# A scan re-ordered by pairs of heads, one convolution tap moved to ScalarE and GpSimd, and a re-ordered opening

## The reference

```python
zxbcdt = u @ in_proj_w.T                      # z 256, x 256, B 2048, C 2048, dt 32 columns
xBC = causal_conv1d(xBC, conv_w, conv_b)      # depthwise, 4 taps: y[l] = sum_k w[k] * x[l - 3 + k] + b
a_log = -softplus(dt); cum = cumsum(a_log)
seg = exp(cum_i - cum_j)
scores = where(tril, seg * einsum('in,jn->ij', C, B), 0)
y = scores @ x                                # per head; plus the state carried between chunks of 128
y = y + D * x;  out = (y * silu(z + z_bias)) @ out_proj_w.T
```

## Time and profile before

| | us |
|---|---|
| median of 3 runs | 1198.76 (1198.08 to 1199.36) |
| the profiled execution's own time | 1198.02 |
| its span, first to last instruction | 1196.3 |

### The profile page before, as it was taken

One profiled execution on the slowest core, in us unless ns is written; L12 is line 12 of the kernel. 1 busy time (PEld: TensorE's weight loads), 2 busy tenths in 40 slices (PEclk: granted clock), 3 DMA queues, 4 the chain that ended last, 5 costly groups with the idle time before them and its releaser, 6 DMA issues.

```text
span 1196.3 us, 18801 instructions
## 1 busy us (share of the span) xinstructions
PE 1043.1 (87%) x6632; PEld 634.3 (53%) x6632; DVE 847.9 (71%) x1864; ACT 518.6 (43%) x1125; POOL 251.7 (21%) x519
## 2 busy tenths in 40 slices
PE   3999898798999898988999998998998998976556
PEld 1444445554444656654444666654445576555345
DVE  4999724578999665678999646789998546765138
ACT  1766521246766311446666211446665212421134
POOL 3222100032222010132221011132221001224432
PEclk9999999899999999999999999999999999988778
DMA  5789400002434000004333000004336304034546
GB/s 191 262 272 278 146 1 18 1 2 92 133 119 127 11 1 19 18 2 133 120 126 102 2 0 18 19 5 160 122 120 175 94 1 124 2 93 117 182 148 233
DMA packets 74255, 113.27 MB, mean 95 GB/s; under 512 B 5944, under 2 KB 64192, under 8 KB 73266
## 3 DMA queue, kind: packets, MB, share of 16 engines
q1 hardware_dynamic: 70322, 100.08, 27.0%
q10 hardware_dynamic: 2304, 8.39, 2.0%
q0 software_dynamic: 1536, 3.60, 1.0%
HBM read 93.38 MB, written 19.27 MB: 94 GB/s over the span
## 4 chain that ended last, share of the span: by engine, by line
PE 60%; DVE 20%; issue 8%; ACT 7%; POOL 2%; another core or an unknown queue 1%; DMA 1%; DVEq 0%; POOLq 0%; SPq 0%; ACTq 0%
PE bank L902 24%; DVE hf L1688 6%; PE bank L967 4%; PE bank L1145 3%; PE bank L1053 3%; PE bank L1187 3%; PE bank L1069 3%; DVE u L1924 2%; PE bank L915 2%; PE bank L1231 2%; PE bank L1234 2%; PE bank L982 2%; PE bank L893 2%; POOL rs L1536 2%; PE bank L1286 1%
## 5 line engine op out<-in xcount | busy, mean ns | idle before, releaser
L902 PE MATMUL bank<-uT,w_in 128*128 128x512 f32 (+1 forms) x584 | 284.2, 614 | 15.9 <-DVE hf L1688 11.5
L1688 DVE SCALAR_TENSOR_TENSOR hf<-bank,conv_w,hf 128x510 f32<-128x510 f32 (+2 forms) x384 | 277.7, 743 | 16.4 <-ACT hf L1392 11.1
L902 PEld LDWEIGHTS bank<-uT,w_in 128*128 128x128 f32 (+1 forms) x584 | 99.7, 187 | 112.1 <-issue 78.5
L1392 ACT ACTIVATE hf<-bank,conv_b,conv_w 128x512 f32<-128x512 f32 x128 | 99.3, 776 | 135.2 <-PE bank L902 135.2
L1536 POOL TENSOR_TENSOR rs<-ve,half 128x2 f32<-128x2 f32 x56 | 38.9, 695 | 305.5 <-DVE ve L1824 305.3
L1053 PE MATMUL bank<-hf 64*128 64x256 f32 x512 | 90.3, 429 | 12.6 <-issue 7.2
L902 PE MATMUL bank<-uT,w_gu 128*128 128x512 f32 x224 | 99.0, 593 | 0.0
L2108 DVE TENSOR_REDUCE nmax<-bank 128x2 f32<-128x256 f32 (+1 forms) x128 | 65.4, 553 | 20.3 <-PE bank L1234 18.1
L1372 ACT ACTIVATE xc<-bank 128x512 f32<-128x512 f32 x44 | 26.3, 597 | 117.4 <-PE bank L902 77.1
L1053 PEld LDWEIGHTS bank<-hf 64*128 64x128 f32 x512 | 39.1, 186 | 69.9 <-issue 63.6
L1924 DVE TENSOR_TENSOR turned_p<-dec,bank 128x768 f32<-128x768 f32 x64 | 60.9, 952 | 15.9 <-PE bank L1054 4.8
(11 more groups left out here) (306 smaller groups left out, 2050.9 us busy)
## 6 DMA issues: line engine op xcount, KB each, us to landing
hf<-cum_dram SPq DMA_DIRECT2D x32, 384.0 KB, 3.6
dec<-cum_dram SPq DMA_DIRECT2D x32, 384.0 KB, 3.6
tmp<-cum_dram SPq DMA_DIRECT2D x32, 384.0 KB, 3.5
x<-cum_dram SPq DMA_DIRECT2D x32, 384.0 KB, 3.5
y_dram<-xf SPq DMA_DIRECT2D x16, 512.0 KB
hf<-y_dram ACTq DMA_DIRECT2D x16, 512.0 KB, 4.9
w_in<-in_w_in SPq DMA_DIRECT2D x1, 3584.0 KB, 11.7
w_in<-in_w_egu SPq DMA_DIRECT2D x6, 512.0 KB, 9.3
```

The source lines that it names most:

```text
L902: mm = pe.matmul(plan[key][0:n, :], w[:, k, cols], uT[:, k, :], start=k == 0, stop=k == DC - 1)
L1392: act.activation(dst, plan[key][:, :], ACT.Identity, bias=conv_b[:, j:j + 1], scale=conv_w[:, j, TAPS - 1:TAPS]).then_inc(tap0.sem, 1)
L1688: ins = dve.scalar_tensor_tensor(d, x, conv_w[:, j, TAPS - 1 - s:TAPS - s], d, ALU.mult, ALU.add)
```

## The change

Scan. TensorE goes by pairs: the products of both sequences, both projections of pair p + 2, and behind an odd pair both `add_y`. VectorE does the C taps of pair p + 1 ahead of the first multiplication of pair p, and the B taps of pair p + 2 behind the second. For C chunks of pairs 2 to 14 the last tap (s = 3) leaves VectorE: ScalarE writes w[0]·x to a buffer `last_product` (`tap_product`), and GpSimd adds it to `bc` once VectorE is done with taps 1 and 2; VectorE's tap 2 then drains the bank (`tap_and_drain`). TensorE waits for that add before it uses the chunk. Pair 15 keeps three taps on VectorE.

Opening. GpSimd clears `x_pad`, `before` and `table` before the powers, the others behind u. The two halves of u are turned into banks 6 and 7. VectorE clears `zeros_bf` first, and TensorE multiplies zeros 16 times before it turns u. ScalarE runs one small exponential at once (so that its table is loaded), and the waits for `consts_cast` come later.

```diff
         for j in range(2):
-            plan.use(("T", "mix", j), 6, -1)
+            plan.use(("T", "mix", j), 6 + j, -1)
...
             pe.wait_ge(consts_in, 144)
+            pe.wait_ge(*plan.before(("T", "mix", 0), -1))
+            pe.wait_ge(zeros_ready, 1)
+            pe.wait_ge(ahead_var.sem, ahead_var.at(0, 1))
+            for n in range(16):
+                pe.matmul(plan.of(("T", "mix", 0), -1)[:, :], zeros_bf[:, 0:P], zeros_bf[:, :], start=True, stop=True)
             for j in range(2):
                 transposes(pe, "mix", 0, u, j, -1)
-            pe.wait_ge(consts_cast, 1)
...
-                for g in range(2 * PAIRS):
+                def states_times_queries(g):
...
+                for p in range(PAIRS):
+                    for w in range(2):
+                        if p < PAIRS - 1:
+                            pe.wait_ge(*plan.drained(("BC", p, w), r))
+                            if w == 1 and p >= 2:
+                                pe.wait_ge(conv_sum.sem, conv_sum.at(r, p - 1))
                     if p + 2 < PAIRS:
-                        if p + 2 == PROJ_PAIRS[1] and b == 0:
+                        for b in range(2):
+                            states_times_queries(2 * p + b)
+                        if p + 2 == PROJ_PAIRS[1]:
                             pe.wait_ge(w_proj[2], 16)
-                        project_bc(p + 2, b)
+                        for w in range(2):
+                            project_bc(p + 2, w)
+                        if p % 2 == 1:
+                            for b in range(2):
+                                add_y(p, b)
...
+            act.wait_ge(pads_zero, 1)
+            act.activation(empty[:, 0:TILES], half[:, :], ACT.Exp)
             for j in range(2):
                 turned("mix", j, -1, 2)
+            softplus(0)
             act.wait_ge(consts_cast, 1)
-            softplus(0)
...
+                def tap_product(p):
+
+                    key = ("BC", p, 1)
+                    if p > 2:
+                        act.wait_ge(conv_sum.sem, conv_sum.at(r, p - 2))
+                    x = plan[key][:, :].rearrange("p (b l) -> p b l", b=SEQS)[:, :, 0:SEQ - TAPS + 1]
+                    act.activation(last_product, x, ACT.Copy, scale=conv_w[:, 18 + p, 0:1]).then_inc(tap3.sem, 1)
...
                         first_tap(("BC", p + 2, b), bc[:, (p + 2) % 3, b, :], 2 + 16 * b + p + 2)
+                        if b == 1 and p + 2 < PAIRS - 1:
+                            tap_product(p + 2)
...
+                    p = g // 2
+                    if g % 2 == 1 and 2 <= p < PAIRS - 1:
+
+                        pool.wait_ge(tap3.sem, tap3.at(r, p - 1))
+                        pool.wait_ge(*plan.drained(("BC", p, 1), r))
+                        settle(pool)
+                        x = bc[:, p % 3, 1, :].rearrange("p (b l) -> p b l", b=SEQS)[:, :, TAPS - 1:SEQ]
+                        pool.tensor_tensor(x, x, last_product, ALU.add).then_inc(conv_sum.sem, 1)
...
+                def all_taps(p, w):
+                    if w == 1 and p < PAIRS - 1:
+                        dve.wait_ge(tap3.sem, tap3.at(r, p - 1))
+                        tap(r, 1, [bc_chunk(p, w)], taps_done)
+                        tap_and_drain(r, 2, *bc_chunk(p, w))
+                        return
+                    for s in range(1, TAPS):
+                        tap(r, s, [bc_chunk(p, w)], taps_done)
```

More of the change, by code:

```diff
@@ L389, in sandwich @@
         pads_zero = sem("pads_zero")
+        zeros_ready = sem("zeros_ready")
         PADS = 7
@@ L1074, in add_y @@
                                           skip_group_check=True).then_inc(y_added.sem, 1)
-                for g in range(2 * PAIRS):
+                def states_times_queries(g):
                     p, b = steps[g]
[L1078 to L1081, removed]
                     pe.wait_ge(*plan.before(("CB", p, b), r))
-                    for second in [products(n) for n in ns]:
+                    for second in [products(n) for n in (2 * g, 2 * g + 1)]:
                         mm = second()
                     mm.then_inc(plan.fills(("CB", p, b)), 1)
+                for p in range(PAIRS):
[4 more added lines that the diff above has]
+                                pe.wait_ge(conv_sum.sem, conv_sum.at(r, p - 1))
                     if p + 2 < PAIRS:
-                        if p + 2 == PROJ_PAIRS[1] and b == 0:
+                        for b in range(2):
+                            states_times_queries(2 * p + b)
+                        if p + 2 == PROJ_PAIRS[1]:
                             pe.wait_ge(w_proj[2], 16)
-                        project_bc(p + 2, b)
-                    if g == 1:
+                        for w in range(2):
[3 more added lines that the diff above has]
+                                add_y(p, b)
+                    else:
+                        b = p - (PAIRS - 2)
+                        for i in range(2):
+                            g = 2 * (PAIRS - 2) + 2 * b + i
+                            if b == 0 and i == 1:
+                                for w in range(2):
+                                    pe.wait_ge(*plan.drained(("BC", PAIRS - 1, w), r))
+                            states_times_queries(g)
+                            if b == 1 and i == 0:
+                                add_y(*steps[g - 1])
+                    if p == 0:
                         for c in range(DC):
@@ L1695, in tap, with tap_and_drain @@
                         ins.then_inc(plan.drains(key), 1)
+            def tap_and_drain(r, s, key, dst, j):
+                dve.wait_ge(chain, last_tap[0])
+                d = dst.rearrange("p (b l) -> p b l", b=SEQS)[:, :, s:SEQ]
+                x = plan[key][:, :].rearrange("p (b l) -> p b l", b=SEQS)[:, :, 0:SEQ - s]
+                dve.scalar_tensor_tensor(d, x, conv_w[:, j, TAPS - 1 - s:TAPS - s], d, ALU.mult, ALU.add)\
+                    .then_inc(plan.drains(key), 1)
             last_tap = [0]
@@ L1916, in _ @@
                     p, b = steps[g]
+                    d = 2 * g % 4
+                    if g % 2 == 0 and 1 <= g // 2 <= PAIRS - 2:
+                        all_taps(g // 2 + 1, 1)
                     dve.wait_ge(decayed.sem, decayed.at(r, 2 * g + 2))
@@ L1928, in _ @@
                         tap(r, TAPS - 1, [bc_chunk(1, w) for w in range(2)], taps_done)
[L1929 to L1933 removed]
+                    if g % 2 == 1 and g // 2 + 2 < PAIRS:
+                        all_taps(g // 2 + 2, 0)
                 output(1, slice(SEQ, GROUP), 64)
```

33 lines of the change are left out of this document (15 added, 18 removed).

## The result

| | us | ratio to before, 95% interval |
|---|---|---|
| before, median of 3 | 1198.76 (1198.08 to 1199.36) | |
| changed kernel, median of 4 | 1161.36 (1159.64 to 1164.04) | 0.9688 [0.9675, 0.9701] |
| forecast | 1165 (1154 to 1181) | |

The changed kernel is 3.1% faster, 37.4 us by these medians (37.2 when before's fourth run, 1198.43, is counted).

The account below looks back on a forecast made before the run. TensorE was taken as the bound, VectorE as a near second. From 1198.02 us, 25.8 for the scan and 7.5 for the opening left 1164.7; with 0.7 for the median 1165.4, say 1165, range 1154 to 1181.

Parts of the forecast that it names:

- Scan, the stretch: Four scan steps (two pairs of heads), bound by TensorE, fall from 13.04 to 11.92 us, 1.12 less.
- a sign of being wrong: In the scan, a four-step stretch above 12.4 us would show the forecast wrong; 11.6 to 12.1 was expected.
- Scan, the ends: First stretch and last pairs (14 and 15) of each scan round: nothing together, bounds −1 and +1 us a round.
- Scan, round 0's DMA: Round 0's scan would want 1.06 of the DMA engines, so 1 us was taken off the gain, bounds 0 and 5.
- ScalarE's loop: Scan, per pair: product, two taps, multiplication, exponentials, next first tap, hand-overs make 5.6 of 5.96 us; 0.35 to spare.
- Opening: Before the scan: earlier u, zeros, table load and second bank gain 7.5 us, bounds 4.8 and 9.6.
- buys the full clock for what follows: Opening: zeros delay u's turning by 2 us but let the first projections take 3.46 instead of 6.32.
- (a): Scan: GpSimd's add blocks VectorE, which needs 13.3 us a stretch; scan gives nothing or −7, total 1198; chance 0.07.
- (b): Scan: ScalarE's product and added semaphores lengthen the 5.6 us loop by 0.6; stretch 12.5, total 1178; chance 0.20.
- (c): Opening: clock not up after the zeros, gain 4.8 us, total 1168; counted inside the forecast's 0.66.
- (d): Scan: GpSimd's add takes over 4.4 us (point of decision), kernel slower than before, about 1233 at 5; chance 0.03.
- (e): Opening gains nothing, as the power's library load stands behind three clears; total 1172, inside the forecast's 0.66.

Follow-up runs that it names:

- pool_x2: Changed kernel with GpSimd adding the product twice in two dependent steps, so the result holds it twice; 1167.18 us, ratio to before 0.9721.
- act_x2: Changed kernel with ScalarE writing the product twice, the second after the first is done; 1176.96 us, ratio to before 0.9833.
- no_zeros: Changed kernel without the products of zeros in the opening; 1144.24 us on the third chip, where before took 1178.89; ratio 0.9704.
- pool_x3: Changed kernel with GpSimd doing add, subtract, add in place of one add, same result; 1198.29 us, ratio to before 1.0002.
- after_again: The changed kernel, unaltered, run once more on the third chip; 1143.12 us where before took 1178.89, ratio 0.9688.
- last_too: Changed kernel with pair 15's C chunk also getting its last tap by ScalarE and GpSimd; 1147.2 us on the third chip, ratio 0.9717.

## Why the prediction was right, and which terms were off

**Scan, the stretch: right.** 11.92 was forecast, 11.89 came, and the chain has the pieces of the sum: a pair of product groups 1.51 (forecast 1.58), eight projections 3.81 and 3.63 (3.65 each), two `add_y` 1.44 (1.46). The experiments bear out that both parts are needed for it: 12.32 and 12.84 with one alone. One stretch a round breaks the forecast: the one with the half of y takes 12.43, above the 12.4 that I had named as a sign of being wrong, and TensorE waits for a tap in it. I had taken the six stretches as alike. It costs 0.54 a round, where before lost 0.21 at the same place.

**Scan, the ends: mis-sized.** I took them as nothing. In round 1, from the first products to the first `add_y`, before took 12.92 and after 11.81, so the first stretch gained 1.1 as well, just above the upper bound of 1; the next six gave 6.6 (forecast 6.7: five gave 1.15 each instead of 1.12, the sixth less), the end nothing.

**Scan, round 0's DMA: wrong sign of caution.** I took 1 us off. My step was that the same bytes in less time would want 1.06 of the DMA engines. A window of round 0 shows them at 0.98 with 309 GB/s, where before had 0.97 with 280, and TensorE without a gap. So the busy share was no measure of the room left:

```profile
82.00:98.00 16.00, 16.00 (x131) 9.00 (x124) 14.70 (x21) 12.51 (x30) 7.11 (x14) 1.00 0.98 309
```

pool_x2 shows that the caution had its place: with 1.4 us more on GpSimd the same rows of cum hold TensorE up.

**What I had no term for: the clock at the end of the scan.** TensorE waits 1.9 us there for pair 15's taps (in before 1.81); VectorE's last of six taps in a row ends at 368.03, TensorE goes on at 368.14. Behind the wait the granted clock sometimes falls. The same group in round 1 and in round 2 of the changed kernel, timelines of TensorE:

```profile
370.16 0.64 PE L1079 MATMUL bank<-turned_p,x_pad 128*32 128x256 f32 x8 [0.29 <-DVE turned_p L1991]
...
624.09 1.08 PE L1079 MATMUL bank<-turned_p,x_pad 128*32 128x256 f32 x8
```

The window 624 to 628 has a granted clock of 0.64, 370 to 374 has 1.00. The changed kernel had the fall in rounds 2 and 3, before in round 0 alone: its second group of products there takes 1.13 (timeline of before), in round 1 0.63.

```profile
139.36 1.13 PE L1053 MATMUL bank<-hf 64*128 64x256 f32 x4
```

That is what sets round 0 (8.87 saved) and rounds 2 and 3 (6.4, 6.65) off from round 1 (7.71): with the fall a scan is 1.1 to 1.3 longer. In sum the four scans gave 29.6 instead of 25.8.

**VectorE, ScalarE, GpSimd: right.** VectorE 10.74 (10.6 to 10.9), ScalarE 9.59 (10.2 at most), the product 0.67 (0.6 to 0.8), the add 1.27 (1.2). "Up to about 2.5 us cost nothing": two adds, 2.7 with the hand-over, cost nothing in round 1's regular stretch but 5.5 us over the four scans. "The stretch reaches 13.04 again only with an add of about 4": 13.2 at 4.17. ScalarE's loop was called the tightest. act_x2 shows that a loop through ScalarE is, with 0.72 more per stretch for 1.38 more work in it, so 0.66 were covered (forecast 0.35 a pair, 0.7). That these agree is partly luck: the loop that its chain shows has TensorE's projections in it in place of VectorE's multiplication.

**Opening: right to 0.75, partly for the wrong reason.** 7.5 forecast, 8.25 came. u ended at 12.7 and the zeros at 14.0 instead of 14.7. The projections started at 15.4, not 16.7, and took 4.13, not 3.46. Both parts of my step "buys the full clock for what follows", and then 3.46, were off. The 3.46 was misread, for that row in round 3 is not of the same shape. It belongs to the feed-forward's first projections (`w_gu`), which all write 128 rows. On the timeline of before it reads:

```profile
929.12 3.62 PE L915 MATMUL bank<-uT,w_gu 128*128 128x256 f32 x16
```

Those of the opening go by fours between 32 rows (dt) and 128 (x). At the full clock their fours start 0.95, 1.06 and 0.98 apart, against 0.87 in round 3, and this is most of what lies between 3.62 and 4.13. And the clock did not have to be bought. The weight loads show the clock, one after another; the granted clock of the windows reads 1.00 throughout. First before, the timeline of the weight loads:

```profile
23.25 1.36 PEld L915 LDWEIGHTS bank<-uT,w_in 128*128 128x128 f32 x4 [0.81 <-issue]
...
26.66 0.73 PEld L915 LDWEIGHTS bank<-uT,w_in 128*128 128x128 f32 x4 [0.41 <-issue]
```

The changed kernel, inside its zeros, which start 0.43 apart up to 12.17 and 0.21 apart from 12.55:

```profile
12.17 0.15 PEld L952 LDWEIGHTS bank<-zeros_bf 128*128 128x128 bf16 x1 [0.28 <-issue]
12.55 0.96 PEld L952 LDWEIGHTS bank<-zeros_bf 128*128 128x128 bf16 x5 [0.23 <-issue]
```

And no_zeros, inside its projections:

```profile
16.09 0.73 PEld L920 LDWEIGHTS bank<-uT,w_in 128*128 128x128 f32 x4 [0.43 <-issue]
```

Four loads take 1.36 at 1.2 GHz and 0.73 at 2.4. Before reached the full rate between 24.6 and 26.7, the changed kernel at 12.6 in its zeros, no_zeros by 16.1 in its projections. Before had stopped TensorE for 2.36 between its two turnings (for the copy of the shared bank, with the table load ahead of it), as the timeline of before shows:

```profile
20.39 1.08 PE L893 MATMUL bank<-ident,u 128*128 128x128 f32 x4 [2.36 <-ACT uT L1352]
```

Without this stop the work itself does what the zeros were for. That it was the stop which held the rate down is argued from these traces; no run puts the stop alone back. Sixteen zeros save 0.9 in the turning and 0.5 in the projections and delay the turning by 1.2: nothing is left. What the opening gains can be read from no_zeros against before: 4.3 by u's early end (first turning at 12.60 instead of 16.94), 2.4 between the first turning and the projections (2.06 instead of 4.46: second bank and table) and 1.8 in the projections (4.61 instead of 6.39), 8.5 in all. None of the three was run alone.

**Rivals.** (a) falls: taps 0.744. (b) falls for this kernel, but act_x2 made it come true with nearly its numbers (0.6 a loop, stretch 12.5, 1178; measured 0.69 put in, 12.61, 1176.96). (c) falls: the clock was up within the zeros. (d) falls: one add takes 1.27. Its point of decision was put at 4.4; pool_x3 is level with before at 4.17, so it lies near 4.2. (e) falls.

**The tail.** 3.8 of the gain were given back in the profiled execution. Windows from the last down-projection to the end; the granted clock is the third number from the end. Before:

```profile
971.80:1196.30 224.50, 162.49 (x1340) 120.19 (x1340) 121.63 (x380) 63.34 (x146) 64.07 (x95) 0.89 0.39 120
```

The changed kernel:

```profile
934.04:1162.30 228.26, 167.76 (x1340) 123.48 (x1340) 121.72 (x380) 63.45 (x146) 64.18 (x95) 0.87 0.38 118
```

And after_again, the same kernel on the third chip:

```profile
934.12:1141.20 207.08, 159.20 (x1340) 118.50 (x1340) 121.88 (x380) 63.32 (x146) 64.05 (x95) 0.92 0.42 130
```

Instructions and the other engines' work are the same; TensorE's work takes 5.3 longer in the second at a lower clock. The median of the four is 2.7 below the profiled execution, so it probably contains less of it; only one execution has a trace. Why the clock differs there was not tried. The prediction had no term for the tail, and this is luck: the scans gave 3.8 more than forecast and the tail took 3.8 back, so that the profiled execution came at 34.0 saved where 33.3 was forecast. The stretch, not the total, is what bears the prediction out.

## What to carry to other kernels

Where two engines are near the bound, look in the chain for what each change alone would meet next: here the order alone made VectorE the bound, the tap alone stayed with TensorE's group changes, and both together gave half as much again as their sum. Put groups of small matmuls of one kind side by side; here the second one of a pair cost 0.15 to 0.2 us less. Work moved to an idle engine is free only by the slack of the whole ring, buffer included, and in the round with the fullest DMA: measure it there, and don't take an end at which an engine waits (pair 15) for one more hop.

## What the runs showed of the hardware

- Behind TensorE's wait of 1.93 us at the end of the scan its clock stayed up in rounds 0 and 1 and fell in rounds 2 and 3 of the changed kernel's profiled execution; behind 1.81 us in before it fell in round 0 alone; behind 2.73 us in last_too it fell in rounds 0, 2 and 3. With the fall a scan took 1.1 to 1.3 us more in these two kernels, and 2.2 in round 0 of last_too.
- TensorE's busy time for the same eight matmuls was 0.64 us at the upper level of the clock and 1.08 at the lower.
- In the opening the windows' granted clock reads 1.00 while instructions run at half rate (1.36 and 0.73 us for four loads): there the durations tell, not that column.
- A group of four projections that changes the width of its output (32 and 128 rows in turn) starts 0.95 to 1.06 us after the one before, four of one width 0.87.
- On the third chip all kernels were 20 us shorter. Up to the tail the changed kernel agreed to 0.1 us (last down-projection at 934.12 and 934.04). ScalarE's waits in the tail for something off the core (20.3 us in four waits, the longest 12.1, in the list of waits of the changed kernel; 17 to 24 us in every profile taken before those of the third chip) are missing in all four profiles of the third. What it waited for the profile doesn't say, and it stays open.
